# Feed-forward first products as three products of high and low halves in a four-layer attention kernel, with the last layer's queries taken from the transposed sum y

## The reference, cut to what matters

```python
# layer 0: causal cross attention (16 heads of 8), then
x = layer_norm(query + attn_out, ln1_g, ln1_b)
ffn = relu(x @ W1 + b1) @ W2 + b2            # 128 -> 512 -> 128
out = layer_norm(x + ffn, ln2_g, ln2_b)
# layer 1: cross attention (16 heads of 8), no norms
x = x + attn_out
h = gelu(x @ W1 + b1, approximate=True)      # 128 -> 512
x = x + (h @ W2 + b2)
# layer 2: a gate over text and pooled context, then a norm
out = (fused - mu) / sqrt(var + LN_EPS) * gamma + beta      # called y in the kernel
# layer 3: cross attention (16 heads of 64) with an RMS norm in front
normed = y * rsqrt(mean(y**2) + EPS) * norm_w
q, k, v = normed @ wq, ctx @ wk, ctx @ wv
return y + softmax(q k^T) v @ wo
```

## Time and profile before

| | |
|---|---|
| time, median of 3 runs | 1524.22 us (1521.26 to 1524.74) |
| the profiled execution's own time | 1523.22 us |
| its span in the trace | 1521.7 us |
| PE busy | 1418.5 us (93%) |
| DVE busy | 1080.6 us (71%) |
| ACT busy | 977.0 us (64%) |
| POOL busy | 488.1 us (32%) |
| mean granted TensorE clock | 0.992 of 2.4 GHz |

### The profile page before, as it was taken

How to read it: one execution, slowest core, us unless ns; L and a number is a source line. 1 busy time by engine, 2 the same in 40 slices (tenths; PEclk the granted TensorE clock), 3 DMA queues, 4 the chain that set the end, 5 groups by cost and what they waited for, 6 DMA issues and landing times.

```text
span 1521.7 us, 48865 instructions
## 1 busy us (share of the span) xinstructions
PE 1418.5 (93%) x20325; PEld 1030.3 (68%) x20325; DVE 1080.6 (71%) x2644; ACT 977.0 (64%) x1877; POOL 488.1 (32%) x522
## 2 busy tenths in 40 slices
PE   4779999999999999999999999999999999999987
PEld 3455766767676676767667676776767667676756
DVE  4558778677786867778676777867687785776743
ACT  2355767667676766767576676767667676665654
POOL 2132523315242341524224252332424233152402
PEclk9999999999999999999999999999999999999998
DMA  4000000000000000000000000000000000000000
GB/s 141 15 2 15 3 8 16 9 16 2 22 3 9 16 9 16 3 22 3 9 16 9 16 3 22 3 9 16 9 16 3 9 16 9 2 3 8 3 8 9
DMA packets 27798, 20.02 MB, mean 13 GB/s; under 512 B 1088, under 2 KB 27200, under 8 KB 27328
## 3 DMA queue, kind: packets, MB, share of 16 engines
q1 hardware_dynamic: 27584, 16.90, 3.8%
HBM read 12.70 MB, written 4.19 MB: 11 GB/s over the span
## 4 chain that ended last, share of the span: by engine, by line
PE 76%; DVE 10%; POOL 5%; ACT 4%; issue 4%; DMA 0%; SPq 0%; ACTq 0%; DVEq 0%
PE bank L731 63%; PE bank L740 13%; DVE negmax L1261 2%; POOL prob L1157 2%; DVE sums L1408 2%; ACT prob L1096 1%; POOL rstd L1144 1%; DVE z L1319 1%; ACT probT L1031 1%; DVE negmax L1402 1%; DVE stats L1305 1%; POOL prob L1137 1%; POOL var_eps L1141 1%; POOL w_low L1128 0%; DVE mv L1310 0%
## 5 line engine op out<-in xcount | busy, mean ns | idle before, releaser
L1137 POOL TENSOR_TENSOR prob<-prob,rinv 128x512 f32<-128x512 f32 x256 | 262.4, 1044 | 369.1 <-DVE rinv L1268 368.7
L740 PE MATMUL bank<-cst,prob 128*128 128x128 f32 x1536 | 221.5, 277 | 14.5 <-POOL prob L1157 9.6
L740 PEld LDWEIGHTS bank<-cst,prob 128*128 128x128 f32 x1536 | 173.9, 141 | 62.5 <-issue 32.7
L1031 ACT ACTIVATE probT<-bank 128x512 f32<-128x512 f32 x256 | 143.8, 598 | 110.3 <-PE bank L740 109.4
L1261 DVE TENSOR_REDUCE negmax<-bank 128x8 bf16<-128x512 f32 x256 | 159.0, 680 | 70.7 <-PE bank L731 70.6
L1157 POOL TENSOR_TENSOR prob<-prob,rinv 128x512 f32<-128x512 f32 x128 | 132.5, 1042 | 230.0 <-DVE rinv L1412 229.7
L1024 ACT ACTIVATE prob<-bank 128x512 f32<-128x512 f32 x256 | 142.0, 608 | 80.3 <-PE bank L731 80.0
L1266 DVE TENSOR_REDUCE sums<-prob 128x8 f32<-128x512 f32 x256 | 169.2, 661 | 12.9 <-ACT prob L1024 11.0
L731 PE MATMUL bank<-negmax,ident_b 128*128 128x512 bf16 x384 | 129.6, 389 | 14.1 <-DVE negmax L1261 8.3
L731 PE MATMUL bank<-wt,Q 128*128 128x128 f32 x1024 | 126.1, 277 | 0.0
L1096 ACT ACTIVATE prob<-bank,rms_rows 128x256 f32<-128x256 f32 x256 | 104.5, 483 | 30.8 <-PE bank L731 30.7
(11 more groups left out here) (155 smaller groups left out, 2968.7 us busy)
## 6 DMA issues: line engine op xcount, KB each, us to landing
x_in<-in_x SPq DMA_DIRECT2D x16, 256.0 KB, 3.0
c_in<-in_ctx SPq DMA_DIRECT2D x16, 256.0 KB, 3.3
out<-y SPq DMA_DIRECT2D x16, 256.0 KB, 2.3
Q<-in_split_weights SPq DMA_DIRECT2D x1, 1536.0 KB, 9.1
wt<-in_weights SPq DMA_DIRECT2D x1, 1024.0 KB, 10.8
wt<-in_weights SPq DMA_DIRECT2D x1, 640.0 KB, 5.9
...
```

Source lines behind the costliest of these rows:

```text
L740: last = nc.tensor.transpose(o[:, k * P:(k + 1) * P], src(k), ident)
L1031: nc.scalar.activation(probT[:, t].rearrange("p s q -> p (s q)"), bank(g, "PT", l, u, t)[:, :], ACT.Identity).then_inc(probT_ready.sem, 1)
L1137: nc.gpsimd.tensor_tensor(pr, pr, ri, ALU.mult).then_inc(norm_ready.sem, 1)
```

## The change

- `h.l.j` becomes a `split_mm` of `W1`'s halves and two new tiles, `x_high` and `x_low`. Step `x_high.l` (ACT) rounds the transposed input of the feed-forward part (`x1T` for layer 0, `fT` for layer 1), step `x_low.l` (POOL) subtracts. Both tiles are shared by the two layers, so `x_high` waits until the other layer's `h` steps are done.
- `W1_0` and `W1_1` move from the plain to the split weights. They are loaded by a DMA of their own, staged in `V3`, rounded by ScalarE and subtracted by GpSimd at the start.
- `lnF.2` transposes `y` instead of `z`, and so waits for `y_beta`. Step `yn` is gone: `yn_high` reads the PSUM bank and scales by `norm_w`, `yn_low` reads the same bank.
- All plans, banks and `TURN` are new. The plan for the middle groups:

```diff
-for _n, _w in [("W1_0", 512), ("W2_0", 512), ("W1_1", 512), ("W2_1", 512), ("wo3", 1024)]:
+for _n, _w in [("W2_0", 512), ("W2_1", 512), ("wo3", 1024)]:
...
-SPLIT_COLS = 3328
+SPLIT = {"Wk0": 0, "Wk1": 128, "wk3": 256, "wv3": 1280, "wq3": 2304, "W1_0": 3328, "W1_1": 3840}
+SPLIT_COLS = 4352
...
-        h.1.0@475.4604 h.1.1@475.9839 h.1.2@476.2834 h.1.3@477.245 f.1.0@480.119 f.1.1@486.6086 f.1.2@487.1416 v3.5@487.6852
+        h.1.1@590.4219 h.1.0@590.9542 h.1.2@591.2124 h.1.3@591.7107 f.1.0@595.973 f.1.1@598.7666 f.1.2@600.563 f.1.3@601.6429
...
             sp.dma_start(w_stage[:, 0:FIRST_SPLIT], split_weights[:, 0:FIRST_SPLIT]).then_inc(split_first_loaded, 16)
-            sp.dma_start(w_stage[:, FIRST_SPLIT:], split_weights[:, FIRST_SPLIT:]).then_inc(split_rest_loaded, 16)
+            sp.dma_start(w_stage[:, FIRST_SPLIT:], split_weights[:, FIRST_SPLIT:LAST_SPLIT]).then_inc(split_rest_loaded, 16)
+            sp.dma_start(w1_stage, split_weights[:, LAST_SPLIT:]).then_inc(split_last_loaded, 16)
...
                 elif kind == "lnF":
                     n, = index
-                    pe.wait_ge(*z_ready(g, n))
-                    transpose4(bank(g, "lnF", n), lambda k: z[n // 2][:, k, :]).then_inc(lnF_filled.sem, 1)
+                    pe.wait_ge(*(z_ready(g, n) if n < 2 else y_ready(g)))
+                    transpose4(bank(g, "lnF", n), lambda k: (z[0], z[0], y)[n][:, k, :]).then_inc(lnF_filled.sem, 1)
                 elif kind == "h":
                     l, j = index
                     if g == 0:
+                        pe.wait_ge(low_last, 1)
                         pe.wait_ge(rest_loaded, REST)
-                    pe.wait_ge(*(ln_out(g, 0) if l == 0 else attout_ready(g, 1)))
-                    mm(bank(g, "h", l, j)[:, :], w(f"W1_{l}", j * P), (x1T[0] if l == 0 else fT[1])[:, :])\
+                    pe.wait_ge(*x_low_ready(g, l))
+                    split_mm(bank(g, "h", l, j)[:, :], w_split(f"W1_{l}", j * P), (x_high[:, :], x_low[:, :]))\
                         .then_inc(h_filled.sem, 1)
...
+                elif kind == "x_high":
+                    l, = index
+                    act.wait_ge(*(ln_out(g, 0) if l == 0 else attout_ready(g, 1)))
+                    if l == 1:
+                        act.wait_ge(*h_filled.whole(g, 0))
+                    elif g:
+                        act.wait_ge(*h_filled.whole(g - 1, 1))
+                    nc.scalar.activation(x_high[:, :], (x1T[0] if l == 0 else fT[1])[:, :], ACT.Identity)\
+                        .then_inc(x_high_ready.sem, 1)
...
                 elif kind == "yn_high":
-                    act.wait_ge(*yn_ready(g))
+                    act.wait_ge(*lnF_filled(g, 2))
                     if g:
                         act.wait_ge(*q3_filled.whole(g - 1))
-                    nc.scalar.activation(yn_high[:, :], ynT[:, :], ACT.Identity).then_inc(yn_high_ready.sem, 1)
+                    nc.scalar.activation(yn_high[:, :], bank(g, "lnF", 2)[:, :], ACT.Identity, scale=v("norm_w"))\
+                        .then_inc(yn_high_ready.sem, 1)
...
+            pool.wait_ge(high_last, 1)
+            nc.gpsimd.tensor_tensor(w_low[:, last], w1_stage, w_high[:, last], ALU.subtract).then_inc(low_last, 1)
...
+                elif kind == "x_low":
+                    l, = index
+                    pool.wait_ge(*x_high_ready(g, l))
+                    nc.gpsimd.tensor_tensor(x_low[:, :], (x1T[0] if l == 0 else fT[1])[:, :], x_high[:, :], ALU.subtract)\
+                        .then_inc(x_low_ready.sem, 1)
...
-                elif kind == "yn":
-                    dve.wait_ge(*lnF_filled(g, 2))
-                    if g:
-                        dve.wait_ge(*yn_high_ready(g - 1))
-                    nc.vector.tensor_scalar(ynT[:, :], bank(g, "lnF", 2)[:, :], yn_scale[:, 0:1], yn_scale[:, 1:2],
-                                            ALU.mult, ALU.add).then_inc(yn_ready.sem, 1)
                 elif kind == "yn_low":
                     dve.wait_ge(*yn_high_ready(g))
-                    nc.vector.tensor_tensor(yn_low[:, :], ynT[:, :], yn_high[:, :], ALU.subtract)\
+                    nc.vector.scalar_tensor_tensor(yn_low[:, :], bank(g, "lnF", 2)[:, :], v("norm_w"), yn_high[:, :],
+                                                   ALU.mult, ALU.subtract)\
                         .then_inc(yn_low_ready.sem, 1)
```

More of the change, by code:

```diff
@@ L224 @@
[L224 to L229 removed]
+        xT@437.4208 cT@438.6544 q.0@457.0293 k.0@460.1782 S.0.0@464.0121 shift.0.0.1@465.4973 shift.0.0.0@466.419
@@ new lines @@
+        f.1.3@601.6266 v3.7@602.2652 v3.4@603.1509 v3.2@604.1417 ag@605.5921 k3.0@605.807 gp@606.1994 k3.6@610.0881
+        k3.5@611.2122 v3.5@613.6869 v3.6@614.1627 lnT.2@615.0057 k3.3@615.3096 k3.7@615.6439 k3.4@617.0514 v3.1@618.0291
+        v3.0@619.6737 k3.2@620.1072 v3.3@620.2608 lnF.2@622.9223 q3.2@625.4701 q3.3@628.1927 q3.0@629.8923 q3.1@633.7201
+        q3.4@635.0624 q3.7@636.0245 q3.5@636.8234 rows@636.9801 q3.6@637.0221 S3.0@639.3689 shift3.0.0@639.7951
+        shift3.0.1@640.5401 S3.1@645.4895 shift3.1.1@646.6521 shift3.1.0@647.0075 PT3.0.0@647.0177 PT3.0.1@647.1846
@@ new lines @@
+        f.1.3@601.8607 v3.2@602.3521 v3.1@604.1024 ag@604.514 v3.5@606.2663 gp@606.3659 v3.4@608.4023 k3.7@609.1998
+        k3.4@609.5237 k3.6@611.2471 v3.6@612.5234 lnT.2@614.0261 k3.0@614.1916 k3.2@615.3682 v3.0@616.6647 k3.3@616.8869
+        k3.5@619.7632 v3.3@621.484 v3.7@621.5601 lnF.2@621.6103 q3.4@629.5708 q3.2@629.6145 q3.0@632.5943 q3.1@632.6561
+        q3.5@634.4714 q3.3@634.6939 q3.7@635.4963 q3.6@635.7437 rows@636.4635 S3.0@638.3544 shift3.0.0@638.9384
+        shift3.0.1@641.2311 S3.1@642.9933 shift3.1.1@644.6181 shift3.1.0@645.0245 PT3.0.0@646.5461 PT3.0.1@647.6487
@@ new lines @@
+        ag@645.0353 k3.2@647.7393 gp@656.2846 v3.7@657.0028 v3.4@658.0251 k3.7@663.3299 v3.0@663.7104 v3.3@665.5238
+        v3.2@666.3627 lnT.2@667.0369 v3.5@673.8967 k3.1@676.5338 k3.5@678.1565 v3.1@680.6774 k3.4@680.6948 v3.6@683.6381
+        lnF.2@684.367 k3.6@684.7323 q3.6@686.0369 q3.4@701.0884 q3.7@701.0933 q3.3@702.5427 q3.1@706.316 q3.0@706.9848
+        q3.2@710.3573 q3.5@715.7731 rows@716.7686 S3.0@724.7717 shift3.0.0@731.7696 shift3.0.1@732.9206 S3.1@733.3591
+        shift3.1.1@735.063 PT3.0.0@739.0023 shift3.1.0@748.5271 PT3.0.1@750.3953 S3.2@750.928 O3.0@752.934
@@ L405, in __call__, with whole @@
         return self.sem, self.place[index, group] * self.parts + part + 1
-    def whole(self, group):
-        return self.sem, (max(n for (_, g), n in self.place.items() if g == group) + 1) * self.parts
+    def whole(self, group, *start):
+        return self.sem, (max(n for (index, g), n in self.place.items()
+                              if g == group and index[:len(start)] == start) + 1) * self.parts
     def before(self, group, *index):
@@ L524, in xattn_sequence_kernel @@
         y = sb("y", [P, CH, P])
-        ynT = sb("ynT", [P, TOK])
+        x_high = sb("x_high", [P, TOK], F32R)
+        x_low = sb("x_low", [P, TOK], F32R)
         yn_high = sb("yn_high", [P, TOK], F32R)
@@ L590, in xattn_sequence_kernel @@
         ln_out = Signal(sem("ln_out"), "ACT", "ln_out")
+        x_high_ready = Signal(sem("x_high_ready"), "ACT", "x_high")
         relu_ready = Signal(sem("relu_ready"), "ACT", "relu")
```

574 lines of the change are left out of this document (285 added, 289 removed).

## The result

The changed kernel takes **1543.65 us** in the median of 4 runs (1542.09 to 1548.93), the kernel before 1524.41 on the same chip (1521.26 to 1524.74, also 4 runs): a ratio of 1.0147, 95% interval 1.0125 to 1.0169. It is 1.5% **slower**; the forecast had 1497 us. The profiled execution took 1548.93 us, with a span of 1547.0; it is the longest of the four, so its trace shows somewhat more loss than the median has.

The account below looks back on a forecast made before the run. PE's own list, work and waits, was taken to bound the kernel. The terms -21.9 + 8.8 - 3 - 8 - 4 + 1.8 gave -26.3 us, from 1523.2 to 1496.9, forecast as 1497 us; range 1484 to 1512.

Parts of the forecast that it names:

- both signs of being wrong: Wrong if the turn stays above 89.5 us, or if PE's busy time falls by less than 15 us.
- The bound: Whole kernel: PE's own list, work and waits, sets the span; PE idle 2.3 us a turn, in many small waits.
- Part 4: Rest of the new order: waits for probT and half of PT3's for POOL go; -8 us, bounds 0 and -24.
- Part 1: Products of h: 128 split products at 0.687 us instead of 0.858, opening a run set to nothing; -21.9 us.
- Part 2: Longer way to h.1 through x_high and x_low: PE waits 0.55 us a turn, 16 times; +8.8 us.
- Part 3: Around h.0: wait before lnF.0 goes but for 0.2 us, new 0.4 before lnF.2, x_low.0's way adds nothing; -3 us.
- Part 5: The start: first norm at 28.2 instead of 33.65 us, group 0's x_high.0 and x_low.0 take 1.7 back; -4 us.
- rival 2: Around h.0: x_low.0 collides with y_beta over SBUF operands, the later loses up to 0.59 us; 1506 us, chance 0.17.
- rival 5: Slower: x_low.0 stands on POOL behind rstd.2, a late gate delays h every turn; 1546 us, chance 0.05.

Follow-up runs that it names:

- full_products: The changed kernel with x_high, x_low and their waits kept, but full products of the hidden layer; 1559.76 us, ratio 1.0259.
- order_only: The changed kernel's order and bank tables with full products of the hidden layer, without the steps x_high and x_low; 1538.78 us, ratio 1.0122.
- pt_bank: The changed kernel with x_low on VectorE and tile PT.0.0.2 in bank 3 instead of bank 1 in groups 2 to 13; 1534.22 us, ratio 1.0068.
- early_exp: The changed kernel with max, shift and exp of tiles 0.0.1 and 0.0.0 placed earlier in groups 3 to 13; 1537.59 us, ratio 1.0112.
- order_mended: As order_only, with early max, shift and exp of tiles 0.0.1 and 0.0.0, and PT.0.0.2 in bank 3; 1531.62 us, ratio 1.0055.
- y_only: The kernel before, its order kept, with only the queries taken from the transposed y (yn gone, full products); 1530.93 us, ratio 1.0056.

## Why the prediction was wrong

The forecast was a turn of 88.3 us (its own terms give 88.45) and at least 15 us less busy time of PE. The turn is 91.76, and PE's busy time fell from 1418.5 to 1417.5 us: both signs of being wrong came. The products did take 13.7 us off it (1431.2 in full_products), but the order and the steps had put 12.7 on.

- **The bound** was read rightly: PE's list sets the time, and PE's waits are many and small. That was the reason for caution with part 4, and I did not draw it. The 2.3 us of idle time a turn, on which the bounds of part 4 stand, are those of one turn; the mean of twelve is 3.01.
- **Part 1, -21.9.** The mechanism holds, the size was off. In a run of `h` a product starts 0.70 us after the one before it, and 0.77 for the first, not 0.687. Four take 0.77 + 3 x 0.70 = 2.87 us where four full ones took 3.43: 2 x 0.56 = 1.12 us a turn, where the prediction had 1.37. The turn got 1.11 of it, the time 15.2. The openings, which the prediction set to nothing because other runs are joined, are in these 1.12; no run measures the joined ones by themselves.
- **Part 2, +8.8.** PE waits 0.37 before `h.1` (0.44 from start to start, against order_only), where I had 0.55. The number was met by luck. The chain from the start of `o.1` took 747.95 - 743.89 = 4.06 us and not 3.75, mostly since `x_low.1` took 1.28 and not 1.04. It did not show because the cover was 3.62 and not 3.20 in order_only, from `o.1` to `h.1`: it holds 0.42 us of stops of its own, most of it the new wait of `PT.0.0.2` for its bank. In sum PE loses 0.86 us on this way. pt_bank shows the same from the other side: with that wait gone, the wait for `x_low` takes its place.
- **Part 3, -3.** The wait before `lnF.0` went but for some 0.3 us (I had 0.2), and that for y came, 0.30 (I had 0.4). The step that failed is "The way `lnF.0`, `ln_out.0`, `x_high.0`, `x_low.0` ends at about the same time as `lnF.2`, so it adds nothing": it adds 0.50. `x_low.0` took 1.65 to 1.78 us and not 1.04. The way itself was timed well: started at 689.88, an `x_low.0` of 1.04 us would have ended at 690.92, within `lnF.2`, which began at 690.64. The price was wrong. This was the mechanism of rival 2, met by 15 of the 16 `x_low.0`, on top of a subtraction that is 0.23 dearer than a `norm` of itself. Parts 2 and 3 together, as far as they hang on the halves, cost 21.0 us in the runs.
- **Part 4, -8.** This step failed most. I credited the new order with two waits that it takes away and read no wait that it brings. The credit was fair: 7.3 and 2.2 us went, where I had half of 7.3 and 4.3. What came was larger, `S.1.0` with 1.25 us a turn first, and the order and the queries from y cost 1.83 us a turn and 16.6 us in all. But the wait at `S.1.0` is not the whole cause: without it the turn is 0.51 shorter (early_exp), and with the second place mended 0.46 (order_mended). Where the other 1.4 us a turn come from stays open; order_mended has no wait above 0.6 us left that comes back turn by turn. The bounds "0 and -24" had no positive end, although nothing excluded one. y_only shows that in the old order the queries from y cost 7 to 9 us by themselves, 0.3 a turn and the rest in the outer groups. How much of the 16.6 us they are in the new order, no run shows.
- **Part 5, -4.** The order alone did bring the start forward by 3.6 us (first `out` at 196.54). The first `norm` of the changed kernel is at 29.67 (I had 28.2, before 33.65), but its first `out` at 202.59 is later than before: PE waits 1.39 us for the first `x_low`, and its granted clock from 50 to 100 us is 0.80, against 0.90 before, each in one execution. How much of the clock is the kernel's doing is open: the mean clock of the kernel before also goes from 0.984 to 0.997 in its own executions (the last section).
- **The rivals.** The time was near that of rival 5, 1546, which had 0.05, but not its mechanism: `x_low.0` does not wait for `rstd.2`, POOL is idle 2.48 us before it. The chance for slower was too small because all my rivals stood on the two new steps and none on the order.

The first `norm` of the changed kernel, to compare with the earlier trace rows, and its wait for the first `x_low`:

```profile
20.70 6.69 POOL L1158 TENSOR_TENSOR w_low<-Q,w_high 128x3072 fp32r<-128x3072 f32 x1 [19.63 <-ACT w_high L1037]
27.36 2.34 POOL L1161 TENSOR_TENSOR w_low<-V,w_high 128x1024 fp32r<-128x1024 f32 x1
29.67 4.03 POOL L1169 TENSOR_TENSOR prob<-prob,rinv 128x512 f32<-128x512 f32 x4
61.34 0.47 PE L747 MATMUL bank<-x_high,w_high 128*128 128x512 f32 x1 [1.39 <-POOL x_low L1173]
```
